# Thirty-six unread one-number gathers more on POOL, at three places of a four-layer transformer kernel

## The reference, cut to what matters

```
x = x + attention0(norm(x), ctx)      # 16 heads of 8; a score that is exactly 0 is masked
x = x + experts0(norm(x))             # 8 experts, each takes the 128 tokens with the highest probability
x = x + attention1(norm(x), ctx)      # a given mask
x = x + quantised(norm(x))            # gated product on whole numbers, 4-bit weights
x = x + attention2(norm(x), ctx)
x = x + experts2(norm(x))             # 8 experts, one per token
x = x + attention3(norm(x), ctx)
x = x + 4 rounds of 16 experts        # one expert per token and round
```

## Time and profile before

| what | value |
|---|---|
| time, median of 3 runs | 752.91 us (751.76, 752.91, 755.09) |
| the profiled execution's own time | 752.82 us |
| its span, first to last instruction | 751.1 us |
| mean granted clock of PE, of full speed | 0.947 |
| busy | PE 639.7 us, DVE 473.9, ACT 302.9, POOL 213.4 (in 285 instructions) |
| DMA, busy tenths in 40 slices of 18.8 us | 7930016002300000000010116001221121221210 |

### The profile page before, as it was taken

The page is one execution under the profiler, slowest core; times in us unless marked ns, Lnnn a source line. Parts: engine busy times, 40 slices in busy tenths (PEclk is TensorE's granted clock), DMA queues, the critical chain, the costliest instruction groups (busy, mean ns, idle before and its releaser), DMA issues.

```text
span 751.1 us, 17783 instructions
## 1 busy us (share of the span) xinstructions
PE 639.7 (85%) x7124; PEld 391.4 (52%) x7124; DVE 473.9 (63%) x1274; ACT 302.9 (40%) x509; POOL 213.4 (28%) x285
## 2 busy tenths in 40 slices
PE   5888996699899989989996878998889899799793
PEld 3455662377455543646653544566366456365342
DVE  5656758785588678845465745563666665775661
ACT  3223331011443437244423552443357466375362
POOL 6412030220410135141024544201420520520553
PEclk9799988799999999999997998999999999999998
DMA  7930016002300000000010116001221121221210
GB/s 153 307 104 2 1 30 224 15 16 106 119 2 2 1 1 0 1 1 3 2 29 29 27 50 221 2 2 32 69 77 55 51 73 52 58 74 44 58 47 12
DMA packets 44361, 40.41 MB, mean 54 GB/s; under 512 B 12043, under 2 KB 35759, under 8 KB 44152
## 3 DMA queue, kind: packets, MB, share of 16 engines
q1 hardware_dynamic: 39368, 29.87, 12.5%
q0 software_dynamic: 3584, 8.76, 4.6%
q10 hardware_dynamic: 1328, 0.66, 0.3%
HBM read 30.71 MB, written 8.81 MB: 53 GB/s over the span
## 4 chain that ended last, share of the span: by engine, by line
PE 51%; DVE 18%; issue 15%; ACT 6%; DMA 4%; POOL 3%; another core or an unknown queue 1%; DVEq 1%; POOLq 0%; ACTq 0%
PE psum L588 7%; PE psum L598 6%; PE psum L564 4%; PE psum L1857 4%; PE psum L532 3%; ACT scr L359 3%; PE psum L1881 3%; PE psum L1867 2%; DMA scr<-y_d,rowi 2%; PE psum L659 2%; PE psum L799 2%; DVE Mp L455 2%; PE psum L633 2%; PE psum L647 2%; DVE ind L450 2%
## 5 line engine op out<-in xcount | busy, mean ns | idle before, releaser
L359 ACT ACTIVATE scr<-psum 128x1024 f32<-128x1024 f32 x64 | 65.6, 1025 | 99.7 <-PE psum L598 61.3
L1455 ACT ACTIVATE b1r<-big 128x512 f32 x160 | 87.5, 619 | 36.6 <-DVE be L1644 27.8
L455 DVE TENSOR_REDUCE Mp<-psum 128x8 f32<-128x1024 f32 x64 | 77.5, 1223 | 33.1 <-PE psum L588 15.8
L588 PE MATMUL psum<-scr 32*128 32x256 f32 x512 | 90.9, 441 | 7.3 <-ACT scr L359 4.4
L598 PE MATMUL psum<-Qa,scr 32*128 32x128 f32 x1024 | 93.9, 302 | 1.4 <-ACT scr L359 0.6
L532 PE MATMUL psum<-fill,identb 128*128 128x512 bf16 x345 | 90.9, 404 | 0.2
L598 PEld LDWEIGHTS psum<-Qa,scr 32*128 32x128 f32 x1024 | 69.2, 190 | 5.7 <-ACT scr L359 2.2
L335 POOL TENSOR_TENSOR scr<-KT,hmask 128x256 f32<-128x256 f32 x64 | 40.3, 647 | 109.7 <-PE psum L598 71.3
L1781 DVE COPY scr<-psum 128x512 f32<-128x512 f32 x48 | 33.2, 691 | 47.2 <-PE psum L1867 47.0
L588 PEld LDWEIGHTS psum<-scr 32*128 32x128 f32 x512 | 39.5, 190 | 39.9 <-issue 23.4
L1867 PEld LDWEIGHTS psum<-ident,scr 128*128 128x128 f32 x232 | 24.9, 142 | 52.7 <-issue 29.4
(11 more groups left out here) (408 smaller groups left out, 1260.0 us busy)
## 6 DMA issues: line engine op xcount, KB each, us to landing
y_d<-scr SPq DMA_DIRECT2D x36, 130.0 KB
big<-in_L_ffn_W SPq DMA_DIRECT2D x2, 2048.0 KB, 9.1
big<-in_L_ffn_W SPq DMA_DIRECT2D x8, 512.0 KB, 9.2
big<-in_L_ffn_W SPq DMA_DIRECT2D x1, 4096.0 KB, 13.8
b1r<-in_L_ffn_b SPq DMA_DIRECT2D x1, 2048.0 KB, 10.0
scr<-y_d,rowi POOLq DMA_INDIRECT x36, 3.1
scr<-in_ctx SPq DMA_DIRECT2D x1, 512.0 KB, 5.1
x<-in_x ACTq DMA_DIRECT2D x1, 512.0 KB, 5.8
```

Of the source, the lines that this page charges most:

```text
L359: act.activation(PT[i % 2][:, c, :], pair(WU), ACT.Exp, scale=SCALE).then_inc(S(f"exp{c}"), 1)
L455: dve.tensor_reduce(Mp[:, HC * c:HC * c + HC, DH:DH + 1], pair(2 * c).rearrange("p (j k) -> p j k", j=HC), AX.X, ALU.max, negate=True).the ...
L588: ins = pe.matmul(bank[2 * c + s // 2][:, 2 * P * n:2 * P * n + 2 * P], QT[rows, c, i, :], Km[rows, i % KB, c, :, :].rearrange("p v k -> p ...
L1455: ins = act.activation(W2d[d % len(W2d)][:, F * u:F * u + F], W2[k.layer][:, bass.ds(e * F, F)], ACT.Copy)
```

## The change

A new function `pool_aside` issues gathers by indirect DMA of one number for each of the 128 partitions, from the input x with the indices 0 to 127, into a column of a new array `aside` (128 x 36 numbers). Nothing reads `aside`. It is called in layer 0's attention ahead of tiles 4 to 7 (4 gathers each, the first behind a wait for `consts` at 2), in the search behind POOL's last preparation (14), and in layer 1's whole-number stage behind the copy into `lanesx` (6). SP's last instruction becomes a wait for all 36. The array stands ahead of later ones, whose addresses in SBUF move by its size.

```diff
+        aside = sb("aside", [P, 36])
...
+        def pool_aside(pool, first, n):
+
+            for m in range(first, first + n):
+                pool.indirect_dma_start(aside[:, m:m + 1], None, a["x"].rearrange("b p (d o) -> (b p d) o", o=1),
+                                        bass.IndirectOffsetOnAxis(iotp[:, 0:1], 0)).then_inc(S("aside_in"), 16)
+
         def pool_attention(pool, L, tiles):
...
+                if L == 0 and i >= KB:
+                    if i == KB:
+                        pool.wait_ge(S("consts"), 2)
+                    pool_aside(pool, 4 * (i - KB), 4)
                 for c in range(2):
...
             pool.tensor_copy(tv[:, :, :, 4], prest).then_inc(S("tokens_numbered"), 1)
+            pool_aside(pool, 16, 14)
             pool.wait_ge(S("xn_stored"), 16)
...
             pool.tensor_copy(lanesx[:, :, :], lanes[:, :].unsqueeze(2).to_broadcast([P, P, NG]))
+            pool_aside(pool, 30, 6)
             for c in range(1, QC):
...
             sp.wait_ge(S("rows_out"), 16 * (NG8 + NG))
+            sp.wait_ge(S("aside_in"), 16 * 36)
```

## The result

The changed kernel takes 767.42 us (median of four runs, 765.41 to 769.89) against 753.88 of the kernel before beside it (751.76 to 755.09): ratio 1.017, 95% interval 1.0119 to 1.0221, so slower by 13.5 us between the medians, and by 9.0 to 16.7 by the interval. The prediction, 752.8 us and no change, was wrong. The profiled execution took 767.82 us, span 766.1, mean granted clock of PE 0.938 (before: 0.947).

The account below looks back on a forecast made before the run. PE was taken as 51% of the chain that ended last, DVE 18%, POOL 3%. 752.82 us with 0 + (-0.1) + 0 + 0 gave 752.7, and 0.09 for the runs' median made it 752.8 us, range 750.6 to 757.

Parts of the forecast that it names:

- The cost of a gather on POOL: All 36 added gathers: each takes 1.25 us of POOL's time, at most 1.64, together 45 us.
- Layer 0's attention, cost 0: 16 gathers ahead of tiles 4 to 7: keys about 1 us late but written 17.9 us ahead of PE's reading; cost 0.
- The small transfers' share of the DMA engines: Layer 0's attention: 16 transfers of 0.5 KB share the DMA engines with the expert loads, done by 57 us; cost 0.
- The search, cost 0, at most 0.5: 14 gathers taking 17.5 us, at most 23.0, fit in POOL's 24.0 us open before the first index; cost 0.
- its access to PSUM or SBUF: Search: DVE works from PSUM; its SBUF copies beside gathers lose 0.09 us in 1.5; cost 0, at most 0.5.
- The warm first gather, -0.1: Search: first real gather may start 0.6 us sooner and be 0.3 shorter; 0.1 us gain booked, bounds 0 and 0.6.
- Ahead of the whole-number stage, 0: Layer 1: 6 gathers taking 7.5 us, at most 9.8, fit in POOL's 12.51 us idle; cost 0.
- The end and the addresses, 0: SP's final wait is for transfers issued 470 us earlier, and arrays move by 144 bytes per partition; cost 0 each.
- Rival 1: Last two stages: POOL pauses at the descriptors' store from some indirect DMA between 89th and 124th; 752.8 to 761 us; chance 0.12.
- Rival 2: Search: a gather costs over 1.72 us and the cover gives out; at 2.9 us each +16.6 us, 769.4; chance 0.03.
- Rival 3: PE's granted clock falls otherwise between 27 and 100 us: faster, 749.5 to 746.2 us, chance 0.05; slower likewise, 0.02.

Follow-up runs that it names:

- k5_changed: The whole changed kernel timed again, against the kernel before: 730.35 us against 732.47, ratio 0.9989, no late signal.
- k6_pow: The changed kernel with each of the 36 gathers replaced by an unread power of 128 x 5 numbers on POOL: ratio 0.9994 against the kernel before.
- e1_attention: The changed kernel with only the 16 gathers in layer 0's attention kept: ratio 1.0028 against the kernel before.
- k14_changed: The changed kernel alone, timed a third time, on a chip with late signals: 759.13 us against 750.62 for the kernel before, ratio 1.0127.
- e3_whole: The changed kernel with only the 6 gathers ahead of layer 1's whole-number stage kept: ratio 1.0017 against the kernel before.
- k8_late: The kernel before, no added gathers, with delays put into ACT in layer 0's attention and DVE in the search: 740.2 us against 730.6, ratio 1.0115.
- k12_small: The changed kernel plus 96 unread 16-byte transfers issued by SP beside the search: 756.52 us against 750.39 for the kernel before, ratio 1.0114.
- k13_small_alone: The kernel before plus the same 96 small SP transfers, without the added gathers: 748.29 us, ratio 1.0008 against the kernel before.

## Why the prediction was wrong

The cost of a gather on POOL (1.25 us): right, a median of 0.944 to 0.966 us and 0.30 of issue in the traces of the gathers.

Layer 0's attention, cost 0: **the failed step**. Its working holds, tile 5's keys are late and nobody waits for them; k5_changed, k6_pow and e1_attention show that it costs nothing measurable where only that counts. What it left out is that a gather can delay a third party. The step asks who waits for POOL; ACT waits for PE's signal, and beside the second and the fourth row of four gathers, in k14_changed beside the third as well, that comes 1.5 to 2.3 us late. The small transfers' share of the DMA engines, the only side effect that it weighed, isn't the cause: beside tile 7's row, at 62 us, the expert weights are in.

The search, cost 0, at most 0.5: **failed in the same way**. The 14th gather ends at 136.7 us and the first index is read at 147.26, so the cover was ample. DVE wasn't slowed by its access to PSUM or SBUF either: its tests take 1.28 us as before. It waited 1.4 and 2.5 us for PE's signals.

The warm first gather, -0.1: half right. It is 0.94 us long instead of 1.26, but starts 0.76 us behind its index (146.50 and 147.26) where it was 0.89, not 0.3; the time can't show it.

Ahead of the whole-number stage, 0: right on both sorts of chip; no "remote" wait lies beside these six in either trace.

The end and the addresses, 0: right, as far as the scatter lets one tell, by e3_whole (+1.2 us in the middle, -1.0 to +3.5) and by the whole change on chips without late signals (-0.8 and +0.4 us).

Rival 1, a pause at the descriptors' store: no indirect DMA from the 89th to the 124th is longer than those of before; the last eleven are not at 2.9 us. Rival 2: no. Rival 3 named the clock, and its 0.02 for slower was the nearest to what happened; but the clock's fall follows the late signals, as k8_late shows, where they were put in without a gather.

The real failing was in reading. "Another core or an unknown queue 1%" stood in a row that I quoted, on one core, and its places weren't looked up. Each had a PE product that was done, a waiting engine, and a row of back-to-back gathers on POOL beside it. A rival "gathers make PE's signals late, 2 us for each row of four or more on the path" would have given up to four rows in the attention and one long row in the search, so 2 to 10 us, with its evidence in the trace of before.

Which rows make a signal late can be read from the two traces of the changed kernel. In the attention ACT starts 0.96 to 1.08 us after the row's last gather has been issued (43.35 after 42.37, 64.22 after 63.14; 46.37 after 45.37, 57.24 after 56.20, 67.11 after 66.15), if PE's product ended before that. The first row did without a long wait, since PE's product ended 0.5 us behind the row's end in the first trace (33.12 after 32.59, ACT at 33.44) and 2.3 us in the other. The third row did without in the first trace, since the product ended 1.4 us behind the row (53.98 after 52.57), and not in k14_changed, where it ended 0.5 us ahead of it (55.73). So a shift of some us decides how many of the rows cost something.

**Left open.** Why some chips do this. The first pair and chip 3 (k12, k13, k14) do; the other fifteen runs, on six chips, don't. Chip 3 is the only one noted that does, and it wasn't seen otherwise, so whether it is the chip or its state at the time isn't shown. One observation goes along with it: an indirect DMA raises its semaphore in 16 steps, and of these steps the traces of chips with late signals hold 953 of 1,408 (before) and 1,198 and 1,214 of 1,984 (changed), those of the others 1,379 of 1,408 and 1,953 of 1,984. So where signals are late, records of signals are missing as well. The reverse doesn't hold: k13_small_alone's trace has 189 of the 1,536 steps of its small transfers, and no late signal beside them. The Trainium skill ("NOTIFIC — the notification-queue block", "6.4 The other TPB producers" and "7.1 Overflow: three behaviours, one of which stalls the engine") says that each setting of a semaphore can be recorded and that a full path inside the recording block holds its producers back rather than lose a record. By that page the lateness may belong to the recording; no run here shows it, since every run was recorded. A path that holds its producers back and loses nothing would also not explain the missing records. It is a guess, not shown. Nor is shown where the last 4.1 us of the first pair come from: they lie behind real gathers in layers 2 and 3, mostly in the last round, where the changed kernel's trace has two "remote" waits more. Real gathers a little apart, without a wait for the landing, weren't tried.

## What to carry to other kernels

Look up every "remote" or "unknown" wait in a trace of one core before you call a side engine's work free, and compare the starts of those that wait with the ends of what they wait for, since some late signals bear another name: ask not only who waits for that engine, but whose signals were late while it did the same thing elsewhere. When a difference comes out, time the kernel before on the same chip and compare its time with the first one; 730 against 753 us for one program said more than four ratios. A cause that you believe in can be put in by hand, as delays, where the chip doesn't show it.

## What the runs showed of the hardware

- One program takes 752.9 or 750.4 us on some chips and 730 to 733 on others, with equal first 395 us. The difference is in stretches with rows of gathers.
- On the former, PE's signals come up to 3.2 us after its product's end beside back-to-back gathers in the attention and the search (134.83 after 131.66 in k12_small; 139.30 after 136.69 in the first changed trace). In the attention and in layer 3 they are there about 1 us after the row's last gather has been issued (43.35 after 42.37; 64.22 after 63.14; 545.29 after 544.32), in the search not by that measure (139.30 after 136.73, and 134.38 in the midst of the row). DVE's signals to PE in the search aren't late.
- 3 to 5 us after a late signal or a put-in delay of some 2 us began, PE's granted clock fell to 1.2 GHz for 3.4 or 6.8 us (46.2 after 41.1 and 66.6 after 62.2 in the first changed trace, 48.3 after 44.7 in k8_late, 46.2 after 43.2 in k12_small); not after each (in k12_small not after those at 56.09 and 65.97, in k14_changed not after that at 57.24).
- A chain of gathers that each wait for the last one's landing runs at 3.0 to 3.9 us, not at the 2.5 to 3.3 from issue to landing.
